# Twelve-stage transformer mixture, two stages with eight large experts: token rows gathered two experts ahead and behind TensorE's transposes, and a down product moved ahead of the last out product

## The reference, cut to what matters

```
E, H, TOP_K = (8, 176, 2)
xt = layernorm(x).reshape(1024 tokens, 256)
scores = sigmoid(xt @ gate_w.T)                 # 8 experts
top_scores, top_idx = top_k(scores, 2)          # normed, times 2.5
h = einsum('td,edh->eth', xt, w1)
u = einsum('td,edh->eth', xt, w3)
y = einsum('eth,ehd->etd', silu(h) * u, w2)
routed = einsum('td,te->td', y, combine)        # two experts per token
shared = silu(xt @ sw1) * (xt @ sw3) @ sw2      # for every token
x = x + 0.5 * (routed + shared)
```

## Time and profile before

| what | value |
|---|---|
| median of 3 runs | 1899.74 us (1897.71 to 1900.02) |
| profiled execution | 1901.41 us, span 1899.6 us, mean granted TensorE clock 0.906 |
| TensorE (PE) busy | 1580.7 us, 83% of the span |
| VectorE (DVE) busy | 1427.7 us, 75% |
| ScalarE (ACT) busy | 1152.8 us, 61% |
| GpSimd (POOL) busy | 900.3 us, 47% |
| device memory traffic | 83 GB/s over the span |

### The profile page before, as it was taken

How to read it: one execution, slowest core, us unless ns; L and a number is a source line. 1 busy time by engine, 2 the same in 40 slices (tenths; PEclk the granted TensorE clock), 3 DMA queues, 4 the chain that set the end, 5 groups by cost and what they waited for, 6 DMA issues and landing times.

```text
span 1899.6 us, 28348 instructions
## 1 busy us (share of the span) xinstructions
PE 1580.7 (83%) x10286; PEld 1282.0 (67%) x10286; DVE 1427.7 (75%) x2995; ACT 1152.8 (61%) x2383; POOL 900.3 (47%) x914
## 2 busy tenths in 40 slices
PE   6899468978997276789888886889999999999775
PEld 4799346866996145578567765667777777777565
DVE  6788568757886666677786756778888888888755
ACT  4588146654883137821872243788888888888542
POOL 0677432003775610030261053166787777878353
PEclk9999688989998587978997987899999999999888
DMA  8798310513994200000003043001000000000243
GB/s 306 220 290 260 94 42 21 184 39 103 284 297 144 84 23 1 1 1 1 1 1 118 19 133 100 15 9 34 17 23 29 23 18 29 23 12 15 91 126 115
DMA packets 87450, 158.89 MB, mean 84 GB/s; under 512 B 13560, under 2 KB 62840, under 8 KB 86264
## 3 DMA queue, kind: packets, MB, share of 16 engines
q1 hardware_dynamic: 72696, 116.96, 18.6%
q0 software_dynamic: 14592, 39.87, 7.4%
HBM read 124.28 MB, written 32.51 MB: 83 GB/s over the span
## 4 chain that ended last, share of the span: by engine, by line
PE 26%; DVE 12%; POOL 7%; ACT 5%; issue 4%; DMA 1%; another core or an unknown queue 0%; POOLq 0%; SPq 0%; DVEq 0%; ACTq 0%
PE ps L79 24%; POOL work L91 3%; DVE work L91 3%; DVE wt L99 3%; PE ps L83 2%; ACT wt L87 2%; DVE ering L91 2%; POOL work_r L91 1%; ACT L87 1%; DVE wt L91 1%; POOL wt_r L91 1%; DVE X L99 1%; DVE H L95 1%; POOL H L145 1%; ACT ering L87 1%
## 5 line engine op out<-in xcount | busy, mean ns | idle before, releaser
L79 PE MATMUL ps<-work_r 128*128 128x256 f32 (+2 forms) x1200 | 243.5, 294 | 5.7 <-ACT work_r L87 1.5
L79 PE MATMUL ps<-wt,work 128*128 128x256 f32 (+1 forms) x1176 | 232.7, 371 | 9.1 <-ACT work L87 8.5
L79 PE MATMUL ps<-H_r,wt_r 128*128 128x512 f32 x576 | 222.7, 431 | 9.8 <-POOL wt_r L91 7.5
L87 ACT ACTIVATE work<-ps 128x512 f32<-128x512 f32 (+5 forms) x339 | 151.6, 477 | 128.8 <-PE ps L79 73.0
L145 POOL DMA_INDIRECT work<-Hd,work x176 | 169.0, 960 | 127.9 <-DVE work L111 84.3
L79 PEld LDWEIGHTS ps<-wt,work 128*128 128x128 f32 (+1 forms) x1176 | 181.0, 201 | 38.9 <-ACT work L87 9.4
L79 PEld LDWEIGHTS ps<-work_r 128*128 128x128 f32 (+1 forms) x1200 | 190.1, 188 | 20.9 <-DVE work_r L91 11.0
L99 DVE SCALAR_TENSOR_TENSOR wt<-ps,wt 128x511 f32<-128x511 f32 (+2 forms) x234 | 174.4, 747 | 22.5 <-ACT wt L87 16.6
L87 ACT ACT_TABLE_LOAD x113 | 145.0, 1283 | 42.6 <-DVE lmv L119 25.2
L91 POOL TENSOR_TENSOR work<-work 128x256 f32<-128x256 f32 (+2 forms) x164 | 162.1, 996 | 6.5 <-ACT work L87 1.3
L91 DVE TENSOR_TENSOR work<-work,ps 48x256 f32<-48x256 f32 (+3 forms) x242 | 128.1, 530 | 49.0 <-PE ps L79 36.8
(11 more groups left out here) (250 smaller groups left out, 4213.3 us busy)
## 6 DMA issues: line engine op xcount, KB each, us to landing
ering<-in_moe_w SPq DMA_DIRECT2D x87, 624.0 KB, 4.8
ye<-work SPq DMA_DIRECT2D x64, 256.0 KB
wt<-in_ssd_wg SPq DMA_DIRECT2D x64, 128.0 KB, 2.2
ye<-work SPq DMA_DIRECT2D x16, 384.0 KB
Hd<-H SPq DMA_DIRECT2D x32, 128.0 KB, 1.7
ye<-early SPq DMA_DIRECT2D x1, 4096.0 KB, 14.6
wt<-in_ssd_wg SPq DMA_DIRECT2D x8, 512.0 KB, 3.6
work<-Hd,work POOLq DMA_INDIRECT x176
```

The lines of the kernel that those rows point to most:

```text
L79: self.last = self.e.matmul(o, l, r, start=start, stop=stop, skip_group_check=True)
L87: self.last = self.e.activation(o, a, f, **kw)
```

## The change

Two things change, in both stages alike.

First, GpSimd's gathers. Before, it gathers the rows of experts 0, 1 and 2 at the step ("slots",), and at each ("in", e) those of expert e+3; those of expert 4 and up wait until TensorE has transposed the rows of the expert four before, whose buffer they take. After, it gathers the rows of experts 0 and 1 at ("slots",), and at ("in", e) first waits until TensorE has transposed the rows of expert e, and then gathers those of expert e+2. The number of gathers stays at 24 a stage.

Second, the list's end: ("down", 2) stands ahead of ("out", 7), and ("down", 3) right behind it, ahead of the last eight fetches.

```
-            todo += [("mid", 7), ("sum", 0), ("down", 1), ("out", 7)]
+            todo += [("mid", 7), ("sum", 0), ("down", 1), ("down", 2), ("out", 7), ("down", 3)]
             todo.extend(("fetch", t, 0) for t in range(NT))
-            todo += [("sum", 1), ("down", 2), ("down", 3)]
+            todo += [("sum", 1)]
...
             for t in range(NT):
                 g.wait_ge(s_rows, "out", si)
-            if e >= 4:
-                g.wait_ge(PE, "x", si, e - 4, 1)
-            else:
-                g.wait_ge(PE, "table", si)
+            g.wait_ge(PE, "table", si)
             for j in range(NB):
                 g.gather(M5.xs[e % 4][:, j, :], None, Hd, M5.slots[:, NB * e + j:NB * e + j + 1])
...
                 if s[0] == "slots":
-                    for e in range(3):
+                    for e in range(2):
                         g_rows3(g, si, e)
...
                 elif s[0] == "in":
-                    if s[1] + 3 < 8:
-                        g_rows3(g, si, s[1] + 3)
+                    if s[1] + 2 < 8:
+                        g.wait_ge(PE, "x", si, s[1], 1)
+                        g_rows3(g, si, s[1] + 2)
                     if s[1] >= 2:
                         low_weights3(g, si, s[1], "dn")
```

## The result

The changed kernel takes 1883.36 us (median of 4 runs, 1880.20 to 1888.52) against 1899.13 for the kernel before (4 runs, 1897.71 to 1900.02): 15.8 us less, ratio 0.9927 with a 95% interval of 0.9911 to 0.9942. The forecast was 1886.5. The profiled execution has a span of 1878.4 us, mean granted clock 0.909.

A forecast was written before the change was run, and what follows sets the result against it. TensorE's completion signals, held during GpSimd's unbroken gathers, were taken as the bound. Stage 11's 6.8 us plus stage 9's 7.4, less 1, gave 1888.2 profiled, 1886.5 in the median's terms; range for 8 in 10: 1880 to 1900.5.

The forecast's parts named there:

- What held the engines: Stages 9 and 11: TensorE's completion signals are held during GpSimd's unbroken gathers, up to 10 us, and come after the row ends.
- The rival that nothing changes: Stages 9 and 11: late signals have another cause and the release stays at 1831.83; time 1899.7, chance 0.20.
- Expert 2's wait at nothing: GpSimd's wait for expert 0's transposes, ahead of expert 2's gathers, is already met and costs nothing.
- T, "2.7 us behind the row": VectorE's release 2.7 us behind the gather row's end: 1824.55 instead of 1831.83 in stage 11, 1109.55 instead of 1116.42 in stage 9.
- ScalarE's 0.48 us and VectorE's 0.56 behind T: Expert 0's 48-row silu (0.48 us) and product (0.56 us), through earlier before, now come behind the release.
- 6.8 and 7.4 us a stage: Out 1 starts earlier by 6.8 us in stage 11 and 7.4 us in stage 9, together 14.2.
- 1 us off for an unclean release: Taken off the sum of 14.2 us, since the release may come less cleanly than 2.7 us.
- Later gathers cost nothing: Expert loop: rows gathered one expert later still land in time, 7.3 of 11.3 us, so cost nothing.
- The down product costs nothing: Stage end: down 2 ahead of out 7 delays it 1.8 us within 3.0 us of room, expected cost 0.
- The rival on the other side: Stage end: out 7's signals are held in the row of fetches, 6.7 us more a stage; time 1913 or about 1900, chance 0.10.

The follow-up runs named there:

- the row of 15 in two forms: Kernel before, gathers two experts ahead with only the buffer wait, ratio 0.9949; or three ahead, each behind expert e's transposes, ratio 0.9964.
- the breaks: Kernel before with a GpSimd memset ahead of the gathers of experts 3, 4 and 5, in three lengths: ratios 0.9896, 0.9955 and 1.0002.
- the row of 21: Kernel before with expert 5's rows gathered once more behind the 18 gathers of each of the two stages: 1906.22 us against 1901.19, ratio 1.0031.
- the long ones: Kernel before with a 128x1024 memset on GpSimd ahead of the gathers of experts 3, 4 and 5: 1878.82 us against 1901.19, ratio 0.9896.
- the repeat: The changed kernel run once more, nothing altered, beside new runs of the kernel before: 1886.58 us against 1897.43, ratio 0.9945.
- the row of 18: The kernel before, unchanged, with 18 gathers in an unbroken row in stages 9 and 11: 1899.13 us.
- the wait in stages 0 and 2: Second token tile's gathers wait for the shared expert's last gate and up products: 1881.55 us on the changed kernel, 1878.50 on long memsets.

## Why the prediction was right, point by point

- **What held the engines** (signals held during a row of gathers): right in the main. It stands on the row of 15 in two forms and on the breaks; the row of 21 bears it out in stage 9 and by the length of stage 11. "Come after the row ends" is too strong: ScalarE's start at 1827.57, which the prediction itself cites, is ahead of the row's end at 1829.12.
- **The rival that nothing changes**, for which the Trainium skill's "SBUF — State Buffer", section "Who interferes with whom", speaks: out. The experiments with breaks change only GpSimd's steps, and each stage is 10 us shorter with the long ones. The rule tells of ports; these runs don't show that a port is at work, only that a rule on ports isn't the whole of what GpSimd's gathers do to others.
- **Expert 2's wait at nothing**: not so, but of little weight. I had that wait met before its turn. It left a gap of 0.84 us in stage 11 (1.24 in stage 9), and so broke the row after six gathers. Whether this break lets expert 0's 48-row block through in time differs: in the first profile of stage 11 ScalarE starts on it at 1807.38, 14.2 us behind the first gather, in the repeat (ScalarE, then VectorE) 15.6 us behind it, and the stage is shorter by 7.9 and 8.0 us alike:

```profile
1813.77 0.49 ACT L87 ACTIVATE work<-ps 48x384 f32<-48x384 f32 x1 [2.12 <-PE ps L83]
```
```profile
1815.24 0.56 DVE L91 TENSOR_TENSOR wt<-work,ps 128x384 f32<-128x384 f32 x1 [0.40 <-PE ps L79]
```

- **T, "2.7 us behind the row"**: this is the term that was mis-sized most, and the first reason that the stages gained more than forecast. In stage 11 I had T 18.2 us behind the first gather (1824.55 - 1806.35); measured 17.1, in both profiles. The row's end was 0.3 us later than I had it (15.80 instead of 15.5), the release 1.3 us behind it (1.35 in the repeat) instead of 2.7. In stage 9 18.55 were forecast; measured at most 15.7 (both of VectorE's products stand in a group that begins at 15.1), and 17.26 in the repeat, and out 1 there is 2.6 and 1.6 us sooner than forecast. A distance near 2.7 us (2.5 to 2.8) fits the rows of 15 and 18, not the shorter ones and not the row of 21.
- **ScalarE's 0.48 us and VectorE's 0.56 behind T**: wrong. In all four stages profiled the 48-row block was done before T. From T to out 1 it took 9.06 us in stage 11, 9.4 forecast; out 1 started 8.3 us sooner than before, 6.8 forecast. TensorE had 2 us of idle time ahead of out 0 in the forecast, and has none that its row shows.
- **6.8 and 7.4 us a stage**: 7.9 (66.00 - 58.09) and 9.7 (66.91 - 57.20); in the second profile of the same kernel 8.0 and 8.7. I took 1 us off for an unclean release; that was the wrong way.
- **Later gathers cost nothing**: right. TensorE's transposes of experts 3 to 7 wait for no rows.
- **The down product costs nothing**: right, 0.9994. Out 7's copy starts 4.2 us behind the first fetch (1855.43 - 1851.26) instead of 2.9, 1.3 later where 1.8 were forecast, and the 16 fetches have no gap:

```profile
1850.52 3.62 PE L79 MATMUL ps<-wt,work 128*128 128x256 f32 x16
1851.26 0.95 POOL L145 DMA_INDIRECT H<-ye,get  x1 [8.12 <-DVE wt L91]
1855.43 1.02 DVE L111 COPY work<-ps 128x512 f32<-128x512 f32 x2 [2.26 <-issue]
...
1861.53 0.95 POOL L145 DMA_INDIRECT work<-ye,get  x1 [0.30 <-issue]
```

- **The rival on the other side** (the tail turns on out 7) is out with that. One signal in this row was late, and harmless: down 3's matmuls end at 1855.76 + 1.89 = 1857.65, and VectorE's sum on it starts at 1859.78, after 0.41 us of wait for "remote".
- **The whole against the two stages.** The two stages give 17.6 us in the first profile, the medians 15.8, and the repeat's runs 10.4 by the ratio. So it is in part luck that the forecast came as near as it did: the two stages gave 17.6 and 16.7 us, where 14.2 were forecast, and the whole kernel 15.8 in one set of runs and 10.9 in another. The profile's 21.2 us has 3.6 us from stages that are the same in both; in the repeat 16.7 of the stages' own stand against 16.3 of the span. Neither sum is as quiet as it looks: at stage 9's first gather the two profiles are already 5.8 and 5.1 us ahead of the profile before (3.7 and 4.7 of it TensorE's shorter wait in stage 0), and between stages 9 and 11 they lose 2.3 and 5.6. Two parts of that loss can be read: TensorE's clock falls at other places. Behind stage 9, before and in the first profile after:

```profile
1205.00:1240.00 35.00, 31.07 (x145) 24.04 (x146) 27.93 (x44) 29.17 (x52) 11.22 (x10) 0.95 0.09 24
```
```profile
1189.30:1227.10 37.80, 32.60 (x145) 25.47 (x146) 28.16 (x45) 29.20 (x52) 11.23 (x10) 0.91 0.08 22
```

In stage 10's end, the windows before and in the repeat:

```profile
1772.00:1784.00 12.00, 9.68 (x50) 8.28 (x48) 10.11 (x30) 3.32 (x16) 4.62 (x7) 0.78 0.13 44
```
```profile
1761.00:1775.80 14.80, 12.46 (x49) 10.48 (x47) 9.24 (x30) 3.44 (x15) 4.49 (x7) 0.62 0.11 35
```

The third number from the right is the granted clock, 0.95 and 0.91, 0.78 and 0.62 on average over these windows. The same eight matmuls take 1.98 us in the one and 3.76 in the other, the higher and the lower of the two levels (TensorE's timeline, before and repeat):

```profile
1776.38 1.98 PE L79 MATMUL ps<-wt,work 128*128 128x256 f32 x8
```
```profile
1766.16 3.76 PE L79 MATMUL ps<-wt,work 128*128 128x256 f32 x8
```

What makes the clock fall there in one and not in the other I haven't tried; nor does it explain all of the spread between the runs of one kernel (8.3 us in four runs of after).

## What to carry to other kernels

When an engine waits long for a result that its producer has already finished, and the profile names no releaser, look at what GpSimd does then; an unbroken row of indirect DMAs is a candidate. Spread them over the work that needs them, or put a step of about 1 us between every few: here three useless memsets a stage made the kernel 20 us faster. With the wait in stages 0 and 2 in both and beside the same runs of before, they are 3 us ahead of the reordering by the medians; why is not shown, perhaps since they break the row without a wait on the very signals that are held. A wait that is met "just in time" can still break a row; don't count it as nothing. And compare stage by stage: an unchanged stage here moved by up to 5 us between profiles.

## What the runs showed of the hardware that I had not expected

- While GpSimd issues indirect DMAs one every 1.25 us, TensorE's completions reach ScalarE, VectorE and GpSimd late, up to 10 us. With rows of 15 and 18, the rest comes 2.5 to 2.8 us behind the last gather; with the row of 18 ScalarE's, with one row of 21 VectorE's came before the row's end.
- Signals between ScalarE and VectorE are not late in that stretch. Before, in stage 11, VectorE starts 0.04 us after ScalarE's end at 1827.57 + 0.48, and ScalarE 0.02 us after VectorE's, while the last gather runs (VectorE, then ScalarE):

```profile
1828.09 0.56 DVE L91 TENSOR_TENSOR wt<-work,ps 48x384 f32<-48x384 f32 x1 [7.20 <-issue]
```
```profile
1828.67 0.52 ACT L87 ACTIVATE wt_r<-wt 48x384 fp32r<-48x384 f32 x1 [0.62 <-issue]
```

- The gap decides: 0.34 us between gathers gives nothing, 0.71 us 8.5 us in all, 1.14 us 19.8 us, about the whole. What in the chip is shared between the gathers and these signals was not found; I tried neither gathers of other sizes nor other DMAs of GpSimd.
- Memsets on GpSimd, 1.5 us of them behind the row, add nothing to the hold.
